# Edge network on one core: gathering three-part bf16 rows of h in place of rows of the first-layer table

## The chip, the cores and the metric

The kernel runs on one core of a Trainium2 chip (trn2). The metric is the device time of one execution in microseconds. The engines are TensorE (PE, with its weight loads as PEld), VectorE (DVE), ScalarE (ACT), GpSimd (POOL) and the DMA engines, whose transfers are issued from the queues of SyncE (SP), ScalarE and GpSimd.

## What is computed

12,500 nodes have 32 features each; 200,000 edges (src, dst), sorted by dst, have 16 attributes each.

```python
h = relu(layernorm(x))
x_p, x_f = h[src], h[dst]
fwd = concat([x_f, x_p, edge_attr], 1); bwd = concat([x_p, x_f, edge_attr], 1)
flow = relu(concat([fwd, bwd]) @ Wf1 + bf1) @ Wf2 + bf2
total = segment_sum(flow, concat([dst, src]))
x = x + relu(total @ Wn1 + bn1) @ Wn2 + bn2
h = relu(layernorm(x))
x = x + segment_sum(h[dst], src)
```

## The kernel before, in words

Edges are worked through in tiles of 128. Four tiles (U = 4) make a round, four rounds (R = 4) a window of 16 tiles, and there are NI = 104 windows, so 416 rounds. The first NTW = 98 windows bring new edges; the last six hold the tiles by which blocks of 128 nodes that share a tile are counted twice. A schedule, worked out on the chip, says for every tile which rows it takes and which block of nodes it belongs to.

**Start (up to about 150 us).** DVE normalises x into `h` (L1090 to L1104), finds out whether the edges are sorted (L1115 to L1131), makes one-hot digits for a histogram over src (L1150, L1152; PE sums them at L824) and then builds two schedules, k = 1 for dst and k = 0 for src. Each goes in four chunks of 416 columns: PE multiplies (L866, L867), DVE copies three results out (L1201 to L1203), PE may do the next chunk. A few passes over one row follow (L1206 on); `sched_done` tells the others. Beside that a table is built, block group by block group: ACT stages h (L724), PE transposes (L837), ACT copies (L729), PE multiplies with both halves of the first-layer weights (L846), ACT copies 512 columns (L739), SP stores (L374). The table `t2_rows` has one row of 128 float32 (512 bytes) for each node: what the node adds to the hidden layer when it is a source, for both directions. `h` is also split into three bf16 parts, hi, mid and lo, in `h3` (ACT L743, L746, L750; DVE subtracts at L1158 and L1223).

**Edge stage (about 150 to 4324 us).** For each round, SP loads the 128 indices of every tile and the attributes (L395, L397). GpSimd issues four indirect DMAs that gather the rows of `t2_rows` for src into `ring` (L610), and four that scatter the finished records to `records` (L620). Its order is written out: the gathers of round v + 2, then the scatters of round v. DVE makes the one-hot matrix of dst, two rounds ahead; PE transposes it (L914), ACT copies (L756), PE expands h of the dst nodes out of `h3` (L926), ACT copies into rows 0 to 95 of `cmb` (L762). The hidden layer is two float32 matmuls for each tile: the identity with the gathered rows (L943), and `cmb` (96 rows of dst, one of ones, 16 of attributes) with the weights `w3` (L944). ACT applies relu twice, to the half that is summed into dst (L773) and to the half that goes into the records (L778). PE counts positions (L955 to L959), DVE turns them into `pos` (L1275 to L1281), PE sums over dst (L972), DVE adds to `acc` (L1266).

**After it.** The records are read back in order of src and summed (4334 to about 5130 us, PE L1010), the node network runs, h of the second layer is stored to `h_rows` (SP L429), and GpSimd gathers 1568 tiles of its 128-byte rows (L674, 5223 to 7192 us), which PE sums into x (L1072).

The order around the change is set by semaphores. `gather_t2` may begin when the whole table is in DRAM (`t2_written`), `hist_ps` is 2 and `sched_done` is 2, since `ring` lies over the space of h, of the one-hots and of `e0f`. SP issues in its own order: all stores of the table, then the loads of the first edges.

Of the kernel before, what the change touches and what calls it, by code (L numbers as in the profile page):

```python
# [36 lines left out]
U = 4  # L37
# [21 lines left out]
assert NI % 8 == 0 and NTW % 8 == 2 and RG >= NB - 1 + 3 * U  # L59
# [36 lines left out]
def build(nc, x, sd, ea, w12_in, w3_in, wf2e_in, wn1_in, bn1_in, wn2_in, bn2_in, out):  # L96
    with ExitStack() as ctx:
# [17 lines left out]
        t2_rows = dram("t2_rows", [NBP * P, P])  # L115
# [25 lines left out]
        w12 = sb("w12", [P, U, P])  # L141
        w3 = sb("w3", [H3 + 1 + EA, P])
# [12 lines left out]
        ring = ring_flat.rearrange("p (t c) -> p t c", c=P)  # L155
# [3 lines left out]
        rest = ring_flat[:, 2 * LN_:RG * P]  # L159
        acc = sb("acc", [P, NBP, ACC])  # L160
# [24 lines left out]
        ln_tmp = acc_flat[:, B_:B_ + LN_].rearrange("p (b f) -> p b f", f=D)  # L185
# [53 lines left out]
        t2s = cmb_all[:, 0:2, :, :]  # L239
        before_b = ohd_h[:, :, :, :].rearrange("p k u n -> p (k u n)").bitcast(F32)  # L240
        hs, hT = (before_b[:, m * 2 * P:(m + 1) * 2 * P].rearrange("p (k n) -> p k n", k=2) for m in range(2))
# [39 lines left out]
        hs_ready, hsT_ready, hT_ready, tab_ready = sem("hs_ready"), sem("hsT_ready"), sem("hT_ready"), sem("tab_ready")  # L281
        t2s_ready, t2_written = sem("t2s_ready"), sems("t2_written", 2)
# [81 lines left out]
        def _(sp):  # L364
            sp.dma_start(nat[:, :, :], sd[0:E, :].rearrange("(p c) k -> p c k", p=NP)).then_inc(nat_in, 16)
            sp.dma_start(row_next[0:NP - 1, :], sd[0:E, :].rearrange("(p c) k -> p c k", p=NP)[1:NP, 0, :]).then_inc(nat_in, 16)
            for to, of in ((w12[:, :, :].rearrange("p u c -> p (u c)"), w12_in), (w3[:, :], w3_in), (wf2e[:, :], wf2e_in), (wn1[:, :], wn1_in),
                           (bn1c[:, :], bn1_in), (wn2[:, :, :].rearrange("p k f -> p (k f)"), wn2_in), (bn2r[:, :], bn2_in)):
                sp.dma_start(to, of).then_inc(w_in, 16)

            def store_t2(i, first, last):
                for k in range(2):
                    sp.wait_ge(t2s_ready, i * 2 + k + 1)
                    sp.dma_start(t2_rows[bass.ds((i * 2 + k) * (U * P), U * P), :].rearrange("(u p) f -> p u f", p=P),  # L374
                                 t2s[:, k, :, :]).then_inc(t2_written[k], 16)
            rounds_of(sp, NG // 2, store_t2)


            sp.wait_ge(sched_done, 1)
            sp.wait_ge(rearranged, 1)  # L380
            sp.wait_ge(by_d_copied, 16)
            sp.wait_ge(ea_first, 16)
# [4 lines left out]
            def load_edges(i, m, first, sources):  # L387
                if sources:
                    load_sources(i + 1, (m + 1) % 8)
                for r in range(R):  # L390
# [18 lines left out]
            for m in range(8):  # L409
                load_edges(NTW // 8 * 8 + m, m, False, m < NTW % 8 - 1)  # L410
# [37 lines left out]
            for k in range(2):  # L448
                sp.wait_ge(t2_written[k], 16 * (NG // 2))
# [99 lines left out]
        def _(pool):  # L549
# [38 lines left out]

# [7 lines left out]
            for k in range(2):  # L596
# [8 lines left out]
            def gather_t2(s, m, r):  # L605
# [3 lines left out]
                for u in range(U):  # L609
                    nc.gpsimd.indirect_dma_start(  # L610
                        out=ring[:, m * W + r * U + u, :], out_offset=None, in_=t2_rows,
# [21 lines left out]
            edges(0, 9)  # L633
            with pool.Fori(1, NTW // 8) as s:
                edges(s, 9)
# [57 lines left out]
        def _(act):  # L693
# [25 lines left out]
            def stage_h(i, k, first):  # L719

                if not first:
                    act.wait_ge(hsT_ready, i * 2 + k - 1)
                    act.sem_inc(act_tick, 1)
                nc.scalar.activation(hs[:, k, :].rearrange("p (u f) -> p u f", u=U), h[:, bass.ds((i * 2 + k) * U, U), :], ACT.Copy).then_inc(hs_ready, 1)  # L724

            def tables(i, first, last):
                for k in range(2):
                    act.wait_ge(hsT_ready, i * 2 + k + 1)
                    nc.scalar.activation(hT[:, k, :], pb[k][:, 0:P], ACT.Copy).then_inc(hT_ready, 1)  # L729
                if not last:  # L730
                    for k in range(2):
                        stage_h(i + 1, k, False)
                for k in range(2):
                    act.wait_ge(tab_ready, i * 2 + k + 1)
                    act.sem_inc(act_tick, 1)
                    if not first:
                        act.wait_ge(t2_written[k], 16 * i)
                        act.sem_inc(act_tick, 1)
# [765 lines left out]
```

## Time and profile before

| | us |
|---|---|
| median of 3 runs | 9138.04 |
| lowest and highest run | 9131.39, 9163.98 |
| span of the profiled execution, first to last instruction | 7224.1 |
| GpSimd busy in the span | 5197.9 (72%) |
| PE busy | 4419.8 (61%) |
| DVE busy | 3200.3 (44%) |
| ACT busy | 1352.3 (19%) |

The profiled execution has no device time of its own beside its span. The median of the runs stands 1913.9 us above the span; no view says what lies there. In the views a row of a timeline is start, duration, engine, line, operation, destination<-sources and count; in brackets stands the idle time before it and what ended it.

### The profile page before, as it was taken

The page shows a single profiled execution, that of the slowest core. Times are in us where ns is not written, and L with a number is a line of the kernel's source. Part 1 is how long each engine was busy: PE and PEld are TensorE (multiplying, and loading weights), DVE is VectorE, ACT ScalarE, POOL GpSimd, SP SyncE. Part 2 cuts the span into 40 slices and gives each one's busy share as a digit, 9 for nine tenths or more (in the row PEclk, how much of TensorE's full clock was granted, in tenths as well). Part 3 has the DMA queues.
Part 4 walks back from the last instruction along what each step waited for, and adds up shares of the span by engine and source line. Part 5 has one row for each costly group of instructions (what it writes and reads, how often), then busy time and mean ns, then how long its engine had stood idle before and what let it go on. Part 6 is the DMA issues. An engine that isn't in the chain of part 4 may idle for free.

```text
span 7224.1 us, 127054 instructions
## 1 busy us (share of the span) xinstructions
PE 4419.8 (61%) x23241; PEld 3987.8 (55%) x23244; DVE 3200.3 (44%) x15358; ACT 1352.3 (19%) x4288; POOL 5197.9 (72%) x5767
## 2 busy tenths in 40 slices
PE   4666666666666666666666679999733333333333
PEld 3655556555555655555565569999533333333333
DVE  5444444444444444444444466666523232323232
ACT  2222222222222222222222234434200000000000
POOL 2777777777777777777777766666377777777776
PEclk8666676666766666766667785555655555555555
DMA  5222222222222222222222123333111111111111
GB/s 154 43 46 43 43 43 43 43 42 43 42 43 43 42 43 42 42 42 42 43 42 42 41 35 73 71 71 73 30 14 14 14 14 14 14 14 14 14 14 20
DMA packets 1109393, 290.45 MB, mean 40 GB/s; under 512 B 992782, under 2 KB 1058701, under 8 KB 1108518
## 3 DMA queue, kind: packets, MB, share of 16 engines
q0 software_dynamic: 153824, 183.68, 10.7%
q1 hardware_dynamic: 954758, 88.54, 10.3%
q10 hardware_dynamic: 576, 16.16, 0.7%
q14 instruction: 216, 1.77, 0.1%
q8 instruction: 19, 0.31, 0.0%
HBM read 223.49 MB, written 82.32 MB: 42 GB/s over the span
## 4 chain that ended last, share of the span: by engine, by line
POOL 59%; issue 27%; DVE 6%; PE 3%; DVEq 2%; DMA 2%; POOLq 0%; ACT 0%; ACTq 0%; SPq 0%
POOL records L620 21%; POOL ring L674 20%; POOL ring L610 18%; DVE acc L1266 3%; DVEq L331 1%; PE bank L1010 1%; DVE oht L1337 1%; DVE ohd L1337 1%; DVEq L1266 1%; DMA ring<-records 0%; PE bank L943 0%; PE bank L846 0%; DMA row_next<-in_sd 0%; PE bank L944 0%; PE bank L972 0%
## 5 line engine op out<-in xcount | busy, mean ns | idle before, releaser
L620 POOL DMA_INDIRECT records<-rec,pos x1664 | 1650.3, 992 | 526.7 <-issue 507.8
L674 POOL DMA_INDIRECT ring<-h_rows,didx x1568 | 1491.1, 951 | 576.3 <-issue 477.5
L610 POOL DMA_INDIRECT ring<-t_rows,sidx x1568 | 1519.5, 969 | 484.9 <-issue 482.1
L943 PE MATMUL bank<-ring,ident 128*128 x3328 | 1094.3, 431 | 1254.6 <-DMA ring<-t_rows,sidx 1249.8
L943 PEld LDWEIGHTS bank<-ring,ident 128*128 128x128 f32 x3328 | 868.4, 320 | 1309.9 <-issue 1309.8
L1072 PE MATMUL bank<-ring,ohd 128*128 x1664 | 376.2, 402 | 1282.8 <-POOLq L684 1282.2
L1072 PEld LDWEIGHTS bank<-ring,ohd 128*128 128x128 f32 x1664 | 362.9, 330 | 1295.9 <-issue 1295.9
L1275 DVE TENSOR_TENSOR prod<-bank,q_row 128x392 f32<-128x392 f32 x416 | 235.7, 567 | 1895.8 <-PE bank L959 1895.6
L944 PE MATMUL bank<-w,cmb 113*128 113x128 f32 x3328 | 1026.2, 411 | 0.0
L1266 DVE TENSOR_TENSOR acc<-acc,bank 128x65 f32 x3328 | 734.6, 221 | 524.9 <-issue 279.1
L1266 DVE TENSOR_TENSOR xs<-xs,bank 128x32 f32 x1664 | 304.3, 183 | 1384.2 <-PE bank L1072 1371.3
L944 PEld LDWEIGHTS bank<-w,cmb 113*128 113x128 f32 x3328 | 883.0, 324 | 0.0
L773 ACT ACTIVATE rf<-bank 128x256 f32<-128x256 f32 x416 | 159.8, 384 | 2735.3 <-PE bank L944 2733.2
L972 PE MATMUL bank<-rf,ohd 128*128 128x65 f32 x3328 | 453.1, 279 | 9.7 <-ACT rec L778 0.3
L972 PEld LDWEIGHTS bank<-rf,ohd 128*128 128x128 f32 x3328 | 407.9, 193 | 54.4 <-issue 3.1
L1010 PE MATMUL bank<-ring,ohd 128*128 x1664 | 381.7, 421 | 62.4 <-POOL ohd L654 62.0
L1010 PEld LDWEIGHTS bank<-ring,ohd 128*128 128x128 f32 x1664 | 362.9, 330 | 80.7 <-issue 80.7
L802 ACT CAST raw<-ring (+1 forms) x1664 | 312.4, 192 | 478.6 <-DMA ring<-records 337.5
L1010 PE MATMUL bank<-ring,oht 128*128 x1664 | 382.3, 418 | 6.4 <-issue 6.4
L1010 PEld LDWEIGHTS bank<-ring,oht 128*128 128x128 f32 x1664 | 369.2, 332 | 10.7 <-issue 10.6
L1072 PE MATMUL bank<-ring,oht 128*128 x1664 | 374.5, 401 | 0.0
L1072 PEld LDWEIGHTS bank<-ring,oht 128*128 128x128 f32 x1664 | 367.4, 333 | 0.0
(213 smaller groups left out, 6508.9 us busy)
## 6 DMA issues: line engine op xcount, KB each, us to landing
ring<-records SPq DMA_DIRECT2D x104, 536.0 KB, 4.3
rec_i<-by_d_sd SPq DMA_DIRECT2D x1664, 1.0 KB
cmb<-by_d_ea SPq DMA_DIRECT2D x1664, 8.0 KB
records<-rec,pos POOLq DMA_INDIRECT x1664
ring<-t_rows,sidx POOLq DMA_INDIRECT x1568
ring<-h_rows,didx POOLq DMA_INDIRECT x1568, 2.4
by_d_ea<-in_ea ACTq DMA_DIRECT2D x8, 1579.0 KB, 19.1
t_rows<-cmb SPq DMA_DIRECT2D x26, 256.0 KB, 2.2
```

The costliest lines, as they stand in the source:

```text
L610: nc.gpsimd.indirect_dma_start(out=ring[:, m * W + r * U + u, :], out_offset=None, in_=t2_rows, in_offset=bass.IndirectOffsetOnAxis(ap=sid ...
L620: nc.gpsimd.indirect_dma_start(out=records, out_offset=bass.IndirectOffsetOnAxis(ap=pos[:, r, u:u + 1].bitcast(U32), axis=0), in_=rec[:, r ...
L674: nc.gpsimd.indirect_dma_start(out=h2g[:, w * W + t, :], out_offset=None, in_=h2_rows, in_offset=bass.IndirectOffsetOnAxis(ap=didx[:, k, t ...
L773: nc.scalar.activation(rf[:, :, 0:HID], pre[:, :, 0:HID], ACT.Relu)
L802: ins = nc.scalar.copy(pairs[:, bass.ds(j0 + u, 1), :].rearrange("p a k -> p (a k)"), srec[w][:, bass.ds(at[u], 1), HID + 1:REC].bitcast(I ...
L943: nc.tensor.matmul(p, ident[:, :], ring[:, bass.ds(at[u], 1), :].rearrange("p a c -> p (a c)"), start=True, stop=False)
L944: ins = nc.tensor.matmul(p, cmb[:, r, u, :], w3[:, :], start=False, stop=True)
L972: ins = nc.tensor.matmul(pb[3][:, u * ACC:(u + 1) * ACC], ohd[:, r % 2, u, :], rf[:, u, :], start=True, stop=True)
L1010: ins = nc.tensor.matmul(s_bank[r][:, u * ACC:(u + 1) * ACC], s_oh[r][:, u, :], srec[w][:, bass.ds(at[r * U + u], 1), 0:ACC].rearrange("p ...
L1072: ins = nc.tensor.matmul(s_bank[r][:, u * D:(u + 1) * D], s_oh[r][:, u, :], h2g[:, bass.ds(at[r * U + u], 1), :].rearrange("p a f -> p (a ...
L1266: return nc.vector.tensor_tensor(to, to, src[:, u * width:(u + 1) * width], ALU.add)
L1275: placed = chain.link(nc.vector.tensor_tensor(prod[:, :, :], q[:, 0:U, :], bcast_mid(q_row[:, r % 2, :], U), ALU.add))
```

## The change

The table, its weights `w12`, its loop on ACT, PE and SP and its two scratch tiles go. `h3` itself is stored to DRAM as `h3_rows` (96 bf16, 192 bytes a node), each of its three parts by its own DMA as soon as it is split off. GpSimd gathers rows of `h3_rows` into `hring`. PE transposes the four gathered tiles of a round with the bf16 identity into bank 5, ACT copies them into rows 0 to 95 of `cmb` (with the ones and the attributes), and the expanded h of dst goes into a tile of its own, `cmb_dst`. The hidden layer is `cmb_dst` with `wdst` and `cmb` with `wsrc`. GpSimd's order is the scatters of round v, then the gathers of round v + 4 (`LEAD`); the source indices are loaded two windows ahead. It waits for `h3_written` in place of the table and `sched_done`. In the schedule ACT takes the copy of `base_row`, and `blk` is made in one pass over it. On DVE the digits come ahead of the wait for the deviation, the subtractions lie between the one-hots, and the memset of `acc` no longer waits for `lo_ready`.

```diff
-            def store_t2(i, first, last):
...
+            sp.wait_ge(rearranged, 1)
+            sp.wait_ge(by_d_copied, 16)
             load_sources(0, 0)
-            for k in range(2):
-                sp.wait_ge(t2_written[k], 16 * (NG // 2))
+            load_sources(1, 1)
+            for k, part_ready in enumerate((hi_ready, mid_ready, lo_ready)):
+                sp.wait_ge(part_ready, 1)
+                sp.dma_start(h3_rows.rearrange("(b p) f -> p b f", p=P)[:, :, k * D:(k + 1) * D], h3[:, :, k * D:(k + 1) * D]).then_inc(h3_written, 16)
+            sp.wait_ge(sched_done, 1)
+            sp.wait_ge(ea_first, 16)
...
-            for k in range(2):
-                pool.wait_ge(t2_written[k], 16 * (NG // 2))
...
-            pool.wait_ge(mid_ready, 1)
             pool.wait_ge(hist_ps, 2)
-            pool.wait_ge(sched_done, 2)
+            pool.wait_ge(h3_written, 48)
...
-                        m2, r2 = m + (r + 2) // R, (r + 2) % R
+                        m2, r2 = m + (r + LEAD) // R, (r + LEAD) % R
+                        scatter_records(s * 8 + m, r)
                         if m2 < gathers:
-                            gather_t2(s + m2 // 8, m2 % 8, r2)
-                        scatter_records(s * 8 + m, r)
-            gather_t2(0, 0, 0)
-            gather_t2(0, 0, 1)
+                            gather_h3(s + m2 // 8, m2 % 8, r2)
+            for g in range(LEAD):
+                gather_h3(0, g // R, g % R)
...
             nc.scalar.activation(h3[:, :, 0:D], h, ACT.Copy).then_inc(hi_ready, 1)
-            span(act, 1, 8, tables)
             act.wait_ge(r1_ready, 1)
-            nc.scalar.activation(h3[:, :, D:2 * D], ln_tmp, ACT.Copy).then_inc(mid_ready, 1)
...
+            nc.scalar.activation(h3[:, :, D:2 * D], h, ACT.Copy).then_inc(mid_ready, 1)
             act.wait_ge(r2_ready, 1)
+            nc.scalar.activation(h3[:, :, 2 * D:H3], h, ACT.Copy).then_inc(lo_ready, 1)
+            for n, k in enumerate((1, 0)):
+                for c in range(J // JC):
+                    act.wait_ge(sched_ps, n * (J // JC) + c + 1)
+                    nc.scalar.activation(base_row[k][:, c * JC:(c + 1) * JC], pb[6][:, 0:JC], ACT.Copy).then_inc(base_copied, 1)
...
+                act.wait_ge(srcT_ps, v)
+                act.sem_inc(act_tick, 1)
+                nc.scalar.activation(cmb[0:H3, r, :, :].rearrange("p u n -> p (u n)"), pb[5][0:H3, :], ACT.Copy)
                 act.wait_ge(hd_ps, v)
                 act.sem_inc(act_tick, 1)
-                nc.scalar.activation(cmb[0:H3, r, :, :].rearrange("p u n -> p (u n)"), pb[1][0:H3, :], ACT.Copy).then_inc(cmb_ready, 1)
+                nc.scalar.activation(cmb_dst[:, r % 2, :, :].rearrange("p u n -> p (u n)"), pb[1][0:H3, :], ACT.Copy).then_inc(cmb_ready, 1)
...
+            def transpose_sources(i, r, gathered):
+                at = four(pe, gs_row, i * W + r * U, RG - 1)
                 if gathered:
                     pe.wait_ge(gat[r], 16 * U * (i + 1))
                     pe.sem_inc(pe_tick, 1)
+                for u in range(U):
+                    ins = nc.tensor.matmul(pb[5][0:H3, u * P:(u + 1) * P], hring[:, bass.ds(at[u], 1), :].rearrange("p a c -> p (a c)"), ident_h[:, :],
+                                           start=True, stop=True)
+                ins.then_inc(srcT_ps, 1)
...
-                    nc.tensor.matmul(p, ident[:, :], ring[:, bass.ds(at[u], 1), :].rearrange("p a c -> p (a c)"), start=True, stop=False)
-                    ins = nc.tensor.matmul(p, cmb[:, r, u, :], w3[:, :], start=False, stop=True)
+                    nc.tensor.matmul(p, cmb_dst[:, r % 2, u, :], wdst[:, :], start=True, stop=False)
+                    ins = nc.tensor.matmul(p, cmb[:, r, u, :], wsrc[:, :], start=False, stop=True)
...
+                    if not last or r < R - 1:
+                        transposes(j, k)
+                        transpose_sources(j, k, more)
                     counts(i, r, first)
...
-                    nc.vector.tensor_copy(base_row[k][:, s], pb[6][:, 0:JC])
-                    nc.vector.tensor_scalar(blk[k][:, s], pb[6][0:1, 0:JC], 1.0 / P, None, ALU.mult)
                     nc.vector.tensor_copy(e0f[:, s], pb[7][0:1, HCOL:HCOL + JC]).then_inc(sched_read, 1)
                 dve.wait_ge(sched_read, (n + 1) * (J // JC))
+                dve.wait_ge(base_copied, (n + 1) * (J // JC))
+                own.link(nc.vector.tensor_scalar(blk[k][:, :], base_row[k][0:1, :], 1.0 / P, None, ALU.mult))
...
-            dve.wait_ge(lo_ready, 1)
             own.step(nc.vector.memset(acc[:, :, :], 0.0))
```

## Rows read from the trace of the kernel before

**Rows 1.** The page: shares of the chain that ended last, and GpSimd's three groups.

```profile
POOL 59%; issue 27%; DVE 6%; PE 3%; DVEq 2%; DMA 2%; POOLq 0%; ACT 0%; ACTq 0%; SPq 0%
...
L620 POOL DMA_INDIRECT records<-rec,pos x1664 | 1650.3, 992 | 526.7 <-issue 507.8
L674 POOL DMA_INDIRECT ring<-h_rows,didx x1568 | 1491.1, 951 | 576.3 <-issue 477.5
L610 POOL DMA_INDIRECT ring<-t_rows,sidx x1568 | 1519.5, 969 | 484.9 <-issue 482.1
```

**Rows 2.** Waits over the span: engine, tile and line, us in total, times, longest.

```profile
PE bank L943 <- DMA ring<-t_rows,sidx: 1249.8, 390, 4.9
...
POOL records L620 <- DVE pos L1281: 18.9, 11, 2.8
```

**Rows 3.** Timeline, GpSimd: first gather and scatter, last gather and scatter.

```profile
149.84 3.51 POOL L610 DMA_INDIRECT ring<-t_rows,sidx  x1 [7.34 <-issue]
...
167.62 1.04 POOL L620 DMA_INDIRECT records<-rec,pos  x1 [0.30 <-issue]
...
4163.92 1.23 POOL L610 DMA_INDIRECT ring<-t_rows,sidx  x1 [0.30 <-issue]
...
4322.86 0.98 POOL L620 DMA_INDIRECT records<-rec,pos  x1 [0.30 <-issue]
```

**Rows 4.** Timeline, tail: two rounds of PE at full clock without gathers.

```profile
4279.13 0.48 PE L943 MATMUL bank<-ring,ident 128*128 x2
...
4284.53 0.48 PE L943 MATMUL bank<-ring,ident 128*128 x2
```

**Rows 5.** Groups by line: what the added steps are most like.

```profile
L914 PE MATMUL bank<-ident_h,ohd_h 128*128 128x128 bf16 x1664 | 247.8, 299 | 13.6 <-DVE ohd_h L1248 13.4
...
L762 ACT ACTIVATE cmb<-bank 96x512 f32<-96x512 f32 x416 | 246.8, 593 | 445.9 <-PE bank L926 430.1 <-issue 15.7
```

**Rows 6.** Timeline of the start, DVE, ACT and PE.

```profile
47.81 0.21 DVE L1133 TENSOR_SCALAR stat<-stat 128x104 f32<-128x104 f32 x1
...
54.91 0.15 DVE L1135 CAST first_f<-first_i 125x1 f32<-125x1 int32 x1 [6.88 <-DMA first_i<-by_d_sd]
...
56.11 3.62 DVE L1103 TENSOR_TENSOR ring<-ring,stat 128x3328 f32<-128x3328 f32 x1
59.77 1.90 DVE L1104 TENSOR_SCALAR ring<-ring 128x3328 f32<-128x3328 f32 x1
61.58 0.99 DVE L1138 TENSOR_SCALAR acc<-raw 125x1600 int32<-125x1600 int32 x1
...
65.95 3.68 DVE L1150 TENSOR_SCALAR ring<-acc 125x800 bf16<-125x800 bf16 x13
...
67.30 2.97 ACT L743 ACTIVATE h<-ring 128x3328 bf16<-128x3328 f32 x1
...
84.17 4.98 PE L824 MATMUL bank<-acc,ring 125*104 125x64 bf16 x100
```

**Rows 7.** Timeline, DVE: the two schedules and the first round.

```profile
96.58 0.15 DVE L1168 COPY edge_col<-start_col 98x1 f32<-98x1 f32 x1 [7.64 <-PE bank L879]
...
138.29 0.59 DVE L1201 COPY wide<-bank 128x416 f32<-128x416 f32 x1 [2.04 <-PE bank L867]
...
140.78 0.59 DVE L1201 COPY wide<-bank 128x416 f32<-128x416 f32 x1 [0.71 <-PE bank L867]
...
142.60 1.88 DVE L1206 SCALAR_TENSOR_TENSOR ring<-jrow,ring 1x1664 f32<-1x1664 f32 x1
...
152.40 0.17 DVE L1238 CAST sdf<-rec_i 128x8 f32<-128x8 int32 x1
...
158.31 5.69 DVE L1319 MEMSET acc<- 128x6760 f32 x1 [1.36 <-issue]
```

**Rows 8.** Windows (busy by engine, clock, DMA share, GB/s) and DMA issues (KB, landing us).

```profile
70.00:80.00 10.00, 6.16 (x29) 5.92 (x30) 9.96 (x29) 2.96 (x12) 8.60 (x1) 0.68 0.69 201
...
h_rows<-ring SPq DMA_DIRECT2D x1, 1664.0 KB, 13.2
```

More of the change, by code:

```diff
@@ L58 @@
 NTW = TW
-assert NI % 8 == 0 and NTW % 8 == 2 and RG >= NB - 1 + 3 * U
+assert NI % 8 == 0 and NTW % 8 == 2
 assert E % 125 == 0 and JC <= 512 and J % 4 == 0 and NI % SW == 0 and TW < NI - SW and EP >= TW * W * P and EP // P - W < TW * W
@@ L447, in _ @@
             sp.wait_ge(h2_written, 16)
-            for k in range(2):
-                sp.wait_ge(t2_written[k], 16 * (NG // 2))
+            sp.wait_ge(h3_written, 48)
         FB_STEPS = 15
@@ L833, in _ @@
             pe.wait_ge(wflow_ready, 1)
-            def transpose_h(i, k):
-                pe.wait_ge(hs_ready, i * 2 + k + 1)
-                nc.tensor.transpose(pb[k][:, 0:P], hs[:, k, :], ident[:, :]).then_inc(hsT_ready, 1)
-            def tables(i, first, last):
-                for k in range(2):
-                    if not first:
-                        pe.wait_ge(t2s_ready, i * 2 + k - 1)
-                        pe.sem_inc(pe_tick, 1)
-                    pe.wait_ge(hT_ready, i * 2 + k + 1)
-                    for u in range(U):
-                        ins = nc.tensor.matmul(pb[2 + k][:, u * P:(u + 1) * P], hT[:, k, :], w12[:, u, :], start=True, stop=True)
-                    ins.then_inc(tab_ready, 1)
-                if not last:
-                    for k in range(2):
-                        transpose_h(i + 1, k)
             def tile_counts(k):
@@ L928, in expand @@
                 ins.then_inc(hd_ps, 1)
-            def hidden(i, r, gathered):
-                v = i * R + r + 1
+            def transpose_sources(i, r, gathered):
                 at = four(pe, gs_row, i * W + r * U, RG - 1)
@@ L973, in sums, with edges @@
                 ins.then_inc(sum_ready, 1)
-            def edges(i, first, last, gathered=True):
+            def edges(i, first, last, gathered=True, next_gathered=True):
                 for r in range(R):
-                    hidden(i, r, gathered)
-                    if r < R - 1:
-                        transposes(i, r + 1)
-                    elif not last:
-                        transposes(i + 1, 0)
+                    hidden(i, r)
+                    j, k, more = (i, r + 1, gathered) if r < R - 1 else (i + 1, 0, next_gathered)
+                    if not last or r < R - 1:
+                        transposes(j, k)
+                        transpose_sources(j, k, more)
                     counts(i, r, first)
-                    if r < R - 1:
-                        expand(i, r + 1)
-                    elif not last:
-                        expand(i + 1, 0)
+                    if not last or r < R - 1:
+                        expand(j, k)
                     sums(i, r, first)
             pe.wait_ge(ones_set, 1)
+            pe.wait_ge(sched_read, 2 * (J // JC))
+            pe.wait_ge(base_copied, 2 * (J // JC))
+            pe.wait_ge(sched_done, 2)
             transposes(0, 0)
+            transpose_sources(0, 0, True)
             pe.wait_ge(lo_ready, 1)
@@ L1477 @@
     x[0:N] = inputs["x"]
-    w12 = np.zeros((P, U, P), np.float32)
-    for u in range(U):
-        w12[u * D:(u + 1) * D, u, :] = np.concatenate([second, first], axis=1)
-    as_dst = np.concatenate([first, second], axis=1)
+    as_src, as_dst = np.concatenate([second, first], axis=1), np.concatenate([first, second], axis=1)
     twice = np.concatenate([w["bf1"], w["bf1"]])[None, :]
```

130 lines of the change are left out of this document (43 added, 87 removed).

## The prediction

> **What bounds the kernel now.** I read the chain that ended last first, then the groups behind it. GpSimd holds 59% of the chain, and "issue", the 0.3 us between two of its DMAs, most of the next 27%; its three groups of indirect DMAs cost about 0.97 us each plus about 0.31 us of issue [rows 1]. The waits say who waits in the edge stage: PE waits 1249.8 us in 390 rounds, 3.2 us a round, for gathered rows, while GpSimd waits 18.9 us in all for positions [rows 2]. The timeline gives the period: from the first scatter at 167.62 to the last gather at 4163.92 GpSimd does 389 rounds, 10.27 us each, or 1.28 us for each of eight DMAs [rows 3]. So 4 ms of the span hang on how many indirect DMAs GpSimd issues, whatever they carry; 149.84 us lie before the first gather and 158.7 us after the end of the last one (4165.15 to 4323.84), where PE is the bound again: 25 rounds, 6.3 us each, 5.40 at full clock [rows 3, 4].
>
> The number of gathers (1568) and scatters (1664) stays. The change can win only at the start, in the order around it and at the tail, and can lose on the price of one gather or on PE.
>
> **GpSimd's DMAs.** A row shrinks from 512 to 192 bytes. The rows of 128 bytes at L674 cost 951 ns each, those of 512 bytes 969, those of 268 bytes, scattered, 992 [rows 1]. 192 bytes lie among them. I take no change; the ends are -18 ns and +23 ns times 1568, so -28 and +36 us.
>
> **The round on PE and ACT.** Removed: the identity matmul on gathered rows. Added: a float32 matmul of 96 rows in its place (same columns, taken as equal), four bf16 transposes, 0.60 us a round as L914's 247.8 us over 416, and an ACT copy of 0.59 us as L762 [rows 5]. Both together on the chain are 1.2 us, against 3.2 us that PE waits [rows 2]. The cover is GpSimd's period; without it, in the tail, the price shows. There ACT idles 445.9 us over 416 rounds, 1.07 us each, just ahead of the copy for PE's expansion [rows 5], and that is where the new copy goes; PE has the like gap in front of the expansion. So I take zero for the tail, with +0.7 us times 25 rounds = +17 us as the upper end. PE now waits for the gather of round v inside round v - 1, ahead of counts and sums of v - 1; with four rounds of lead GpSimd comes to the scatters of v - 1 some 25 us after that gather, so the wait has nobody behind it. DVE's round, SP's 32 edge loads of a window and the one load of indices stay; they are only issued earlier.
>
> **The order.** Before, 12 gathers stand ahead of the first scatter and 389 rounds of eight follow it. Now 16 stand ahead of it and 388 rounds follow. From the first scatter to the last gather that is one period less: -10.3 us. The tail from the last gather on is set by PE, which starts round 391 then in either case, so its 158.7 us stay.
>
> **The start.** Two chains lead to the first scatter, now at 167.62.
>
> The schedule. DVE is free at 48.0; four digit passes at 0.99 us fill its wait for the deviation and the first edges (which let it go at 54.91), reciprocal and scaling (0.8 + 3.6) follow, the two small passes of `lt`, then relu 1.9: h is ready at 59.0, against 61.7 [rows 6]. ACT's hi copy takes 2.97: 62.2. First subtraction 3.6, one-hots 3.68 + 2.31 = 6.0, second subtraction 3.6 (mid is ready by 69), one-hots 6.0: 81.5. PE's second histogram, 5.0 us [rows 6], ends at 86.6, and the first column of the schedule is read at 86.9 in place of 96.58 [rows 7]. The small operations to the first chunk take 4.4 us without the table between them: 91.3. A chunk takes 2.49 us now, with three DVE copies of 0.59 [rows 7]; two leave, so 1.35, and four take 5.4: 96.7. The ACT copy of `base_row` runs beside the remaining one. The single pass for `blk` (1.0) and three passes (3.9): 101.6. The second schedule: 2.6 + 4.4 for its columns, 5.4 for its chunks, 1.0 for `blk`, and 6.25 of passes (142.60 to 148.85, where the 3.6 us subtraction stood before the loads of the first round at 152.40): 121.3. That is 27.6 us ahead of 148.85. From there the first two rounds' one-hots 4.5, the memset of acc 5.7 without the 1.36 us of wait [rows 7], and 2.1 for the positions: first scatter at 133.6.
>
> The stores. Three stores wait for hi (62.2), mid (69) and lo (78.5). Until about 78 the attribute copies fill the DMA engines (share 0.69 over 70 to 80), so hi hardly moves before. The nearest row is the store of the second layer's h, as many pieces (13,312) of 128 bytes, 13.2 us [rows 8]. At that price three end at 78 + 39.6 = 118. The first gather takes 3.5 us and fifteen more 1.25 each: GpSimd would reach the first scatter at 140. If a piece of half the size cost 60% (8 us), they would end at 102 and the schedule would decide, 133.6. I take 137, nearer to the row than the cheap end is.
> The Trainium skill, "DMA: Bandwidth & Descriptors", section "Why small descriptors are slow", gives a piece a fixed 3 cycles beside one for each 32 bytes: 5 cycles for 64 bytes, 7 for 128, so as an estimate 9.4 us a store; by that the stores end at 106, and the sum would be 3 us better than mine.
>
> GpSimd's own gather for the schedule (L592, rows of the edge list) now starts near 59.5, free of the one-hots, and is not late. The 26 table stores leave SP's queue, and SP's first edge loads stand behind the three big stores: if SP is held until lo is nearly written, they land near 120, just when DVE wants them. That is inside the 3 us I added.
>
> **Sum.** First scatter 167.6 to 137: -30.6. One round less after it: -10.3. Gathers, PE, tail: 0. Together -41 us: span 7183. The execution behind the rows has a span of 7224.1, 1913.9 us below the median of the runs, 9138.0; no view shows those microseconds, and I carry them over unchanged: 9097 us, -0.45%.
>
> **The rivals.**
> The stores are the start. A 64-byte piece could cost twice the 128-byte one: 26.4 each, 79 us, ending at 157; first scatter 179, 11 us later than now, and the round won pays it back: 9138, no change. For it: sub-copies of only 64 bytes have no row. Against: the 128-byte row moves 1664 KB in 13.2 us, 129 GB/s, under the 201 GB/s that the row of 70 to 80 us shows, so pieces already hold it and not bytes.
> The Trainium skill, same page, opening table, wants 512 bytes for a DMA and says that below it the engine reads, modifies and writes; by that rule both the 64-byte stores and the 192-byte gathers are the wrong way, and this rival is its outcome. No row here shows a doubling: the 128-byte gathers cost GpSimd no more than the 512-byte ones [rows 1]. 10%.
>
> The unseen time follows the bytes. 1914 us are 0.40 us for each of 4800 indirect DMAs. If they are moved bytes, weights 1568 x 512, 1664 x 268 and 1568 x 128 become 1568 x 192 in the first: 65% of before, -662 us, time 8435. Against: DMA engines are idle for four fifths of the stage in the profile. 8%.
>
> Slower: PE's round becomes the bound. If the unseen time lies in PE's and ACT's chain of the edge stage (4.6 us a round over 416), then the added transposes count in full, 0.60 x 416 = +250 us, and with the copy +495: 9347 to 9592. It decides when the chain, 10.27 - 3.2 = 7.1 us in the profile and 8.3 after, passes 10.27. For it: PE's clock stands between its two levels, and half clock lengthens every matmul. Against: 2 us of room in the profile. 7%.
>
> That the change does not do what it says I see no way for: the table, its loop and the chunk copies are plainly gone.
>
> **Chances.** A measurement of this kernel can tell about 0.5%, 46 us. The forecast has 75%; its -41 lies just inside that bound, and its terms spread to either side (gathers -28 to +36, stores -3 to +3, tail 0 to +17, runs 16 us apart), so it gives 0.37 faster, 0.35 same, 0.03 slower. The stores give 0.08 same, 0.02 slower; the unseen bytes 0.08 faster; PE 0.07 slower. Together faster 0.45, same 0.43, slower 0.12. The range takes the forecast with the gathers' cheap end and some of the runs' spread, 9045, and on the other side the stores' rival with the runs' spread, 9160; the two large rivals, 15%, lie outside.
>
> **What would show it.** Right: first gather near 115, first scatter near 137, 10.27 us a round in between, about 159 us from the end of the last gather to that of the last scatter, PE's wait moved from the hidden layer to the transposes and near 2.5 us a round. Wrong: a gather above 1.0 us; first gather past 125; GpSimd waiting for positions or relu in the middle of the stage; a tail round above 7 us; or a span that falls by 41 us while the median does something else.

## The result and the profile after

| | median us | runs | span of its profiled execution | its own time |
|---|---|---|---|---|
| before | 9134.72 | 9119.58 to 9163.98 (4) | | |
| after | 9216.57 | 9198.88 to 9231.15 (4) | 9228.1 | 9229.7 |

The ratio is 1.0079, 95% interval 1.0055 to 1.0104: 82 us slower, where -41 was forecast and 9045 to 9160 allowed. The first thing to see is in the table: the span of the changed kernel is its time, within 2 us. Nothing lies outside it. The 1914 us that the profiled execution of before lacked were in no hidden place; here they stand inside the span.

The timeline of after, GpSimd alone, first gather and scatter, last gather and scatter (start us, us; in brackets the idle time before and its releaser):

```profile
112.43 1.00 POOL L597 DMA_INDIRECT ring<-h_rows,sidx  x1 [50.88 <-DMA h_rows<-h]
...
141.49 1.03 POOL L607 DMA_INDIRECT records<-rec,pos  x1 [5.28 <-DVE pos L1229]
...
5654.14 0.95 POOL L597 DMA_INDIRECT ring<-h_rows,sidx  x1 [0.30 <-issue]
...
5901.28 0.98 POOL L607 DMA_INDIRECT records<-rec,pos  x1 [0.30 <-issue]
```

Against [rows 3] the start is as forecast (first gather 112.4 for 115, first scatter 141.5 for 137), and everything after it is longer: 388 rounds of 14.21 us where before had 389 of 10.27. The groups of after say that it isn't the DMAs (busy us, mean ns of one | idle before, by releaser):

```profile
L607 POOL DMA_INDIRECT records<-rec,pos x1664 | 1649.5, 991 | 2139.9 <-DVE pos L1229 1597.5 <-issue 542.5
L597 POOL DMA_INDIRECT ring<-h_rows,sidx x1568 | 1522.6, 971 | 528.7 <-issue 477.8 <-DMA h_rows<-h 50.9
...
L873 PE MATMUL bank<-ident_h,ring 128*96 128x128 bf16 x1664 | 259.7, 300 | 56.5 <-issue 53.2
...
L727 ACT ACTIVATE cmb<-bank 96x512 f32<-96x512 f32 x416 | 246.3, 592 | 393.5 <-remote 314.7 <-PE bank L873 45.2 <-issue 29.2
```

A gather takes 971 ns for 969 and a scatter 991 for 992 [rows 1]. The added transposes take 260 us and the copy 246, as costed. What is new is 1597.5 us in which GpSimd waits for positions; it was 18.9 [rows 2]. The waits of after:

```profile
DVE prod L1223 <- remote: 2315.5, 319, 13.1
...
POOL records L607 <- DVE pos L1229: 1597.5, 301, 10.5
ACT rf L741 <- remote: 1462.0, 153, 18.5
```

So DVE, which makes the positions, waits for the counts of PE, and GpSimd waits for DVE. The experiments had to say whether the change did this.

### The profile page after: what moved, and what is told of

It reads as the page before. It is cut to its first block and busy times, and to the rows that moved or that the text cites. A ratio compares the mean times of both kernels' runs of the same rounds, so it can differ in the third digit from the quotient of the medians.

```text
span 9228.1 us, 130413 instructions
## 1 busy us (share of the span) xinstructions
PE 4739.6 (51%) x24671; PEld 4305.7 (47%) x24674; DVE 3202.2 (35%) x15344; ACT 1577.5 (17%) x4634; POOL 5199.1 (56%) x5767
## 5 line engine op out<-in xcount | busy, mean ns | idle before, releaser
L607 POOL DMA_INDIRECT records<-rec,pos x1664 | 1649.5, 991 | 2139.9 <-DVE pos L1229 1597.5
L597 POOL DMA_INDIRECT ring<-h_rows,sidx x1568 | 1522.6, 971 | 528.7 <-issue 477.8
L886 PE MATMUL bank<-wdst,ring 96*128 96x128 f32 x3328 | 1089.7, 430 | 1240.7 <-ACT ring L730 959.5
L886 PEld LDWEIGHTS bank<-wdst,ring 96*128 96x128 f32 x3328 | 884.6, 325 | 1269.0 <-issue 1268.9
L887 PE MATMUL bank<-wsrc,cmb 113*128 113x128 f32 x3328 | 1037.6, 415 | 0.0
L887 PEld LDWEIGHTS bank<-wsrc,cmb 113*128 113x128 f32 x3328 | 894.4, 328 | 0.0
L1018 PEld LDWEIGHTS bank<-ring,ohd 128*128 128x128 f32 x1664 | 365.8, 329 | 926.2 <-issue 926.2
L1018 PE MATMUL bank<-ring,oht 128*128 x1664 | 393.0, 402 | 765.0 <-issue 574.3
L862 PE MATMUL bank<-oht,h 128*96 128x128 bf16 x1664 | 277.9, 297 | 969.6 <-ACT oht L721 709.9
L1018 PEld LDWEIGHTS bank<-ring,oht 128*128 128x128 f32 x1664 | 372.5, 330 | 780.5 <-issue 780.3
L862 PEld LDWEIGHTS bank<-oht,h 128*96 x1664 | 209.2, 140 | 1049.3 <-issue 1037.2
L730 ACT ACTIVATE ring<-bank 96x512 f32<-96x512 f32 x416 | 246.3, 592 | 1284.1 <-remote 987.4
## 6 DMA issues: line engine op xcount, KB each, us to landing
h_rows<-h SPq DMA_DIRECT2D x3, 832.0 KB, 21.4
```

The lines of the kernel that those rows point to most:

```text
L597: nc.gpsimd.indirect_dma_start(out=hring[:, m * W + r * U + u, :], out_offset=None, in_=h3_rows, in_offset=bass.IndirectOffsetOnAxis(ap=si ...
L607: nc.gpsimd.indirect_dma_start(out=records, out_offset=bass.IndirectOffsetOnAxis(ap=pos[:, r, u:u + 1].bitcast(U32), axis=0), in_=rec[:, r ...
L730: nc.scalar.activation(cmb_dst[:, r % 2, :, :].rearrange("p u n -> p (u n)"), pb[1][0:H3, :], ACT.Copy).then_inc(cmb_ready, 1)
L862: ins = nc.tensor.matmul(pb[1][0:H3, u * P:(u + 1) * P], h3[:, bass.ds(at[u], 1), :].rearrange("p a c -> p (a c)"), oht_h[:, r % 2, u, :], ...
L886: nc.tensor.matmul(p, cmb_dst[:, r % 2, u, :], wdst[:, :], start=True, stop=False)
L887: ins = nc.tensor.matmul(p, cmb[:, r, u, :], wsrc[:, :], start=False, stop=True)
```

## The experiments

The runs come in groups; those of one group ran on the same chip, beside the kernel before. Each recorded expectation stands ahead of its result; it says "call" for such a group.

**The kernel before once more, and parts of the change, first group.** b_same is the kernel before. a_no_srct takes from the changed kernel three things: the transposition of gathered rows, the register load that PE needs for it, and ACT's copy; it leaves the sources' part out of the hidden layer (ones stand there). a_order2 and b_order4 exchange the order of GpSimd's DMAs, and b_order4 loads the source indices two windows ahead, as the changed kernel does. The edits are shown without their lesser lines (...).

```diff
# a_no_srct, after without
-            nc.gpsimd.memset(cmb[H3:H3 + 1, :, :, :], 1.0).then_inc(ones_set, 1)
+            nc.gpsimd.memset(cmb[0:H3 + 1, :, :, :], 1.0).then_inc(ones_set, 1)
...
-                act.wait_ge(srcT_ps, v)
-                act.sem_inc(act_tick, 1)
-                nc.scalar.activation(cmb[0:H3, r, :, :].rearrange("p u n -> p (u n)"), pb[5][0:H3, :], ACT.Copy)
...
-                at = four(pe, gs_row, i * W + r * U, RG - 1)
...
-                for u in range(U):
-                    ins = nc.tensor.matmul(pb[5][0:H3, u * P:(u + 1) * P], hring[:, bass.ds(at[u], 1), :].rearrange("p a c -> p (a c)"), ident_h[:, :],
-                                           start=True, stop=True)
-                ins.then_inc(srcT_ps, 1)
# a_order2, after with
+                        if m2 < gathers:
+                            gather_h3(s + m2 // 8, m2 % 8, r2)
                         scatter_records(s * 8 + m, r)
-                        if m2 < gathers:
-                            gather_h3(s + m2 // 8, m2 % 8, r2)
...
-LEAD = 4
+LEAD = 2
# b_order4, before with the scatter ahead of the gather, LEAD = 4 and load_sources(i + 2, (m + 2) % 8)
```

> The kernel before, profiled once more. The profile of the kernel after has a span of 9228 us with gaps on all queues that the profile of before (span 7224 us, median of the runs 9135 us) does not show. Theory 1 (the 1914 us are ordinary stalls that one lucky execution lacked): a span near 9130 us, GpSimd waiting for positions in the edge stage for 1000 us or more, and an edge stage of 5600 us or more in place of 4174. Theory 2 (the stalls came with the change): a span near 7224 us again, without such waits.

> The kernel after, without the transposition of the gathered rows and without its copy by ScalarE (rows 0 to 95 of cmb hold ones, so the sources' part of the hidden layer is left out). Theory 1 (the chain of PE and ScalarE is the bound of the edge stage, and each added step counts): 1.0 to 1.2 us less in each of 416 rounds, so 400 to 500 us below after, and some 320 to 420 below before. Theory 3 (GpSimd is the bound, the chain has room): within 30 us of after.

> The kernel after with GpSimd's order of before: gathers of round v + 2, then scatters of round v. Theory 1 (chain with stalls, GpSimd waits in 300 rounds): less lead takes room away from the chain, since PE waits for a gather in the middle of the round before: 100 to 400 us slower than after. Theory 3 (GpSimd is the bound): 10 us slower than after, the one round of lead.

> The kernel before with GpSimd's order of after alone: scatters of round v, then gathers of round v + 4, source indices loaded two windows ahead; the table stays. Theory 1 (chain with stalls): four rounds of lead let GpSimd absorb stalls: 50 to 300 us faster than before. Theory 3 (GpSimd is the bound): 5 to 10 us faster than before.

This group showed another speed. The kernel before took 7239.11 us, and so did b_same (ratio 1.0001 [0.9991, 1.0010], span 7218.9). a_no_srct: 1.0001 [0.9992, 1.0011]; a_order2: 0.9997 [0.9988, 1.0007]; b_order4: 0.9993 [0.9984, 1.0003]. So the same program takes 7.2 ms in one group and 9.1 in another, with spans that equal the times in either. I call these the first and the second kind. Theories 2 and 3 had the numbers right here, and yet the groups below show that the kind decided and not the kernel. The span of [rows 1], 7224, is one of the first kind; the result is one of the second.

**The changed kernel on a second chip.** a_same is the changed kernel.

> The kernel after, once more, beside the kernel before on the same chip. Theory 1a (two kinds of execution conditions: with stalls of all queues the kernel before takes 9135 us and the chain of PE and ScalarE bounds the edge stage; without them it takes 7239 us and GpSimd does): where before takes about 7239 us, after takes 7215 to 7265 us, within 0.4% of it, with its first scatter near 140 us, since the 24 us won at the start are given back in the tail or in GpSimd's own time; where before takes about 9135 us, after is again 50 to 110 us slower. Theory 2 (the change itself is slower by 82 us): after is 82 us, 1.1%, slower under either condition.

9194.10 against 9123.81: 1.0087 [1.0071, 1.0103]. Second kind, and the loss repeats.

**Both kernels and two parts on a third chip.** b_again is before, a_again after.

> The kernel before, profiled beside the others of this call. If this chip runs it in about 9130 us: GpSimd waits for positions in 250 rounds or more, the edge stage takes 5500 to 5700 us, its tail after the last gather 210 to 240 us, and all queues show common gaps. If in about 7239 us: as before, none of these.

> After without the transposition and its ScalarE copy, again. Where before takes about 9130 us: by theory 1 (the chain of PE and ScalarE bounds the edge stage there, each added step counts) 250 to 500 us below after, so 180 to 430 below before; by theory 4 (stalls come with the DMAs and the chain has room between them) 0 to 100 us below after. Where before takes 7239 us: within 0.2% of before, as in the first run.

> Before with four rounds of lead, again. Where before takes about 9130 us: by theory 1 50 to 300 us faster than before, since the lead takes up stalls; by theory 5 (the new order is the loss) 50 to 100 us slower than before. Where before takes 7239 us: within 0.2% of it, as in the first run.

> The kernel after. Where before takes about 9130 us: 60 to 90 us slower, as in the two comparisons so far. Where before takes 7239 us: 7215 to 7265 us, with GpSimd's gathers at 0.97 to 1.00 us and the tail after the last gather 10 to 25 us longer than the 159 us of before.

First kind: b_again 7222.6, before 7221.09. a_again took 7210.95, 0.9984 [0.9974, 0.9993]: here the change is a gain of 0.16%. a_no_srct_2: 1.0007 [0.9997, 1.0016], although it has less to do: its gathers took 996 ns each in place of 969, 42 us over 1568. b_order4_2: 0.9992 [0.9983, 1.0002]. The timeline of a_again:

```profile
110.33 1.00 POOL L597 DMA_INDIRECT ring<-h_rows,sidx  x1 [49.07 <-DMA h_rows<-h]
...
139.64 1.04 POOL L607 DMA_INDIRECT records<-rec,pos  x1 [6.08 <-ACT rec L746]
...
4120.61 0.94 POOL L597 DMA_INDIRECT ring<-h_rows,sidx  x1 [0.30 <-issue]
...
4301.20 0.98 POOL L607 DMA_INDIRECT records<-rec,pos  x1 [0.30 <-issue]
```

388 rounds of 10.26 us, as forecast, and PE's wait is at the transposes, 2.1 us a round. In b_again the first scatter stands at 163.2 and the tail takes 158.8 us; here they are 139.6 and 180.6. The two profiles differ by -23.5 at the start, -17.4 from the first scatter to the last gather (one round of 10.3 less, and 0.02 us less in each of the others), +21.8 in the tail and +4.7 behind it: -14, where the medians say -10. The tail is PE's. Its rounds in a_again's timeline, last gathers gone:

```profile
4257.59 0.39 PE L887 MATMUL bank<-wsrc,cmb 113*128 113x128 f32 x2
...
4260.94 0.62 PE L873 MATMUL bank<-ident_h,ring 128*96 128x128 bf16 x4 [0.44 <-issue]
...
4261.68 0.59 ACT L727 ACTIVATE cmb<-bank 96x512 f32<-96x512 f32 x1 [0.55 <-PE bank L873]
...
4263.34 0.59 ACT L730 ACTIVATE ring<-bank 96x512 f32<-96x512 f32 x1 [1.06 <-PE bank L862]
...
4264.43 0.39 PE L887 MATMUL bank<-wsrc,cmb 113*128 113x128 f32 x2
```

6.84 us from hidden layer to hidden layer, where before had 5.40 at full clock [rows 4]; in the mean 7.2 us, where before had 6.3. PE stands 0.44 us "issue" ahead of L873: there the engine loads the ring's slot into a register, which the change put between the two groups of transposes. How much of the tail that is can be read from the windows of the two tails (us, PE, PEld, DVE, ACT and POOL busy, granted clock, DMA share, GB/s) and from PE's waits in them, b_again first:

```profile
4162.44:4321.21 158.77, 125.10 (x942) 109.74 (x942) 113.67 (x541) 57.24 (x147) 106.42 (x108) 0.90 0.14 26
...
PE bank L926 <- ACT oht L756: 16.7, 24, 0.8
```

```profile
4121.56:4302.17 180.61, 146.77 (x1066) 127.48 (x1065) 115.69 (x546) 75.07 (x178) 110.42 (x112) 0.87 0.13 24
...
PE bank L873 <- issue: 7.9, 18, 0.5
PE bank L850 <- DVE ohd_h L1196: 7.7, 18, 0.9
PE bank L862 <- issue: 6.6, 18, 0.5
```

PE is idle for 33.7 us in the one tail and 33.8 in the other, and busy for 21.7 us more: the whole growth is busy time, 15.9 us of it the added transposes. The gap ahead of the expansion (L926 before, L862 after) did shrink, from 16.7 to 7.4 us in all, but new ones opened ahead of the two groups of transposes: 7.9 us for the register load and 7.7 for DVE's one-hots. Without transposes, copy and load the tail takes 148.6 us (a_no_srct_2).

The windows of the edge stage of before, then of a_again show one more thing, and the rounds, 10.27 and 10.26 us, show no cost of it: with the change the clock of the edge stage is 0.53, nearly always the lower level, for 0.69.

```profile
300.00:4100.00 3800.00, 2556.51 (x14050) 2225.74 (x14049) 1713.49 (x8137) 870.04 (x2220) 2898.36 (x2959) 0.69 0.22 43
```

```profile
300.00:4100.00 3800.00, 3006.59 (x15556) 2685.43 (x15557) 1708.92 (x8157) 1090.38 (x2590) 2897.15 (x2963) 0.53 0.18 27
```

**The same on a fourth chip, and the register load.** b_again2 is before; a_early is after with that load ahead of the hidden layer's matmuls.

```diff
+                    if not last or r < R - 1:
+                        at = four(pe, gs_row, j * W + k * U, RG - 1)
                     hidden(i, r)
                     if not last or r < R - 1:
                         transposes(j, k)
-                        transpose_sources(j, k, more)
+                        transpose_sources(j, k, more, at)
```

> The kernel before, for a profile on a chip that runs it in about 9130 us, if this is one. Then: edge stage to about 5800 us (5867.6 in the profile of after, less some 66), GpSimd waiting for positions in 250 rounds or more, gaps on all queues; a tail round near 8 us in place of 8.7. Else a span near 7220 us with a tail of 159 us, as three times before.

> After without the transposition of gathered rows and its ScalarE copy. Where before takes about 9130 us: theory 1 (added steps lengthen the chain in the rounds in which it is the bound, about 300 to 370 of 416, by the 1.0 us that the tail's round shows) 250 to 400 us below after; theory 4 (the chain has room between stalls) less than 100 us below after. Where before takes about 7220 us: within 0.2% of before, with a tail of 149 us.

> Before with the new order and four rounds of lead. Where before takes about 9130 us: theory 1 says the lead takes up stalls and wins 50 to 300 us; theory 5 (the order is the loss) 50 to 100 us slower. Where before takes about 7220 us: within 0.2% of it, as twice.

> After, with TensorE's register load for the gathered rows' slots moved ahead of the hidden layer's matmuls, where it stood before the change; at its new place it leaves TensorE idle for 0.45 us in each round. Theory 6 (that load is the larger part of the longer tail round, 6.4 in place of 5.4 us at full clock): tail 10 to 15 us shorter than after's 181 us, so 0.3 to 0.4% below before where before takes 7220 us; where it takes 9130 us, 100 to 200 us below after by theory 1, 0 to 30 by theory 4.

Second kind: b_again2 9136.81 (before 9118.13), and so at last a profile of before to set beside that of after. Its waits:

```profile
DVE prod L1275 <- remote: 1700.1, 287, 9.1
...
POOL records L620 <- DVE pos L1281: 1501.7, 282, 9.4
```

GpSimd waits 1501.7 us for positions in the kernel **before** too, in 282 rounds. The missing 1914 us, b_again2 against [rows 3]: edge stage from first to last scatter +1491, second layer's gathers +334, end +81, start +6. The change is on top. a_no_srct_3: 0.9910 [0.9888, 0.9933]; b_order4_3: 0.9994 [0.9978, 1.0011]; a_early: 1.0051 [1.0032, 1.0071]. Transposition, copy and register load together make the whole loss and more: 69 us below before without them, 70 above with them (a_same, another chip), by the medians. That is 140 us, less than the 250 to 400 of theory 1 and more than the 100 of theory 4. The order makes none of it, and theory 1's gain from more lead did not come. The load's idle time is gone in a_early (0.6 us ahead of the transposes in all, 56.5 in after); that its place is worth perhaps 30 us is not shown, since a_early and a_same ran on two chips and their intervals touch.

**The transposition behind the counts, and more small loads.** a_mid is a_early with the transposition of the gathered rows behind the counts; b_dbl is before with SP's four 8-byte-row loads of a round issued twice, the second time into a tile that nobody reads.

```diff
# a_mid
                         transposes(j, k)
-                        transpose_sources(j, k, more, at)
                     counts(i, r, first)
                     if not last or r < R - 1:
+                        transpose_sources(j, k, more, at)
                         expand(j, k)
# b_dbl
...
+                    for u in range(U):
+                        sp.dma_start(rec_2[:, r, u, :], by_d_sd[bass.ds(at[u], P), :]).then_inc(twice[r], 16)
```

> After with the register load moved ahead of the hidden layer's matmuls and the transposition of the gathered rows moved behind the counts, into TensorE's wait for ScalarE's copy of the one-hot matrix. Theory 6 (in after the two lengthen the round by their place more than by their work): tail round at full clock back to 5.4 to 5.6 us from 6.4. Where before takes about 9120 us: 60 to 150 us below after, so 0 to 0.8% below before. Where it takes about 7220 us: tail 155 to 165 us, 25 to 35 us below before. If the work itself is the cost (theory 1 in its plain form), the tail round stays above 6.2 us and the time within 30 us of after.

> The kernel before with every load of the 8-byte edge indices issued a second time into a scratch tile (512 more pieces of 8 bytes in a round, DMA packets 1.11 to 1.96 million). Theory 7 (the gaps of all queues come with SP's loads in 8-byte pieces): where before takes about 9120 us, 500 us or more slower; where it takes 7220 us, within 40 us of before, since SP has room. Theory 8 (the gaps come from elsewhere): less than 150 us slower under either condition.

Second kind. a_mid: 9037.57, 1.0016 [1.0006, 1.0025], so most of the loss hung on what stands ahead of the counts in PE's queue. Which of the three steps moved there is the dear one, the four transposes, PE's wait for the gather or the later copy on ACT, no run separates. b_dbl: 1.0075 [1.0058, 1.0093]: +67 us for 1664 DMAs more (1.35 million packets in place of 1.11, not the 1.96 of its expectation). The loads aren't what makes 1914 us.

**Who is late.** The trace answers this without a run. One round of b_again2 (second kind), rows of PE, DVE and ACT:

```profile
2993.70 0.64 PE L944 MATMUL bank<-w,cmb 113*128 113x128 f32 x2
...
3000.97 0.70 PE L959 MATMUL bank<-ohs,ones_h 128*128 128x294 bf16 x3
...
3003.96 0.38 ACT L773 ACTIVATE rf<-bank 128x256 f32<-128x256 f32 x1 [13.17 <-remote]
3004.10 0.57 DVE L1275 TENSOR_TENSOR prod<-bank,q_row 128x392 f32<-128x392 f32 x1 [2.84 <-remote]
```

The like of it in b_again (first kind):

```profile
3006.73 0.64 PE L944 MATMUL bank<-w,cmb 113*128 113x128 f32 x2
3007.40 0.38 ACT L773 ACTIVATE rf<-bank 128x256 f32<-128x256 f32 x1 [6.61 <-PE bank L944]
...
3008.24 0.70 PE L959 MATMUL bank<-ohs,ones_h 128*128 128x294 bf16 x3
3008.98 0.57 DVE L1275 TENSOR_TENSOR prod<-bank,q_row 128x392 f32<-128x392 f32 x1 [4.76 <-PE bank L959]
```

In the latter the hidden layer's record ends at 3007.37 and ACT begins 0.03 us later; counts and DVE likewise. In the former the hidden layer's record ends at 2994.34 and ACT begins at 3003.96 (it waits there for the sums as well, which let DVE go at 2998.24); the counts' record ends at 3001.67 and DVE begins 2.43 us later. Over 350 rounds the delay from the counts' record to DVE is 0.04 us in b_again, 3.8 in b_again2 and 4.7 in after. The trace also holds the updates of semaphores, with gaps. In b_again2, from 474 us to the last gather, those of ACT and DVE come 0.01 us after their instruction in the median. Those of PE come late: 4.6 us for the hidden layer, 3.2 for the transposes, 3.9 for the counts and 0.7 for the expansion, all 0.01 us in b_again. The ends of matmuls are modelled in such a trace, so either PE finishes later than its records say, or its signals are held; the trace can't part the two. In the stage that sums the records, without indirect DMAs, PE's signals come 0.01 us after their records in both kinds; in the second layer's gathers they are late again (1.4 us in the median against 0.01), at a granted clock of 0.50 in both.

**Two theories of that delay.** b_pe8 adds eight matmuls of the added form, twice the change's, without a copy. b_first and a_first put the counts of a round ahead of its hidden layer.

```diff
# b_pe8, before with
+                    for u in range(2 * U):
+                        nc.tensor.matmul(pb[5][0:H3, (u % U) * P:(u % U + 1) * P], h3[:, 0, :], ident_h[:, :], start=True, stop=True)
                     counts(i, r, first)
# b_first (before) and a_first (a_mid)
+                    counts(i, r, first)
                     hidden(i, r)
                     transposes(j, k)
-                    counts(i, r, first)
```

> The kernel before with eight matmuls of the added form (96 columns of weights, 128 columns of data, bfloat16, no signal, nobody waits for them) put into every round ahead of the counts, which is twice what the change adds, and no copy by ACT. Theory 9: on chips of the second kind (9 ms) TensorE really finishes its matmuls 3 to 5 us later than their records say, in the two stages in which GpSimd issues indirect DMAs, so that its work is on the path there: +120 to +300 us on such a chip (twice the added transposes, 2 x 0.60 x 416 = 500 us at most), and the delay from the last count's record to DVE's L1275 grows from 3.6 us. On a chip of the first kind (7.2 ms) nothing within 0.2% (GpSimd's period covers 1.2 us), tail round of PE 6.6 us in place of 5.4. Rival: the transposes cost nothing by themselves and ACT's copy of them, which this kernel lacks, is what the change lost: no change within 0.2% on either kind.

> The kernel before with the counts of a round put ahead of its hidden layer on PE. They are then ready while DVE still adds the sums of the round before. Theory 9a: on chips of the second kind what is late is only the path from PE's counts to DVE (a latency behind the hidden layer's float32 matmuls): the delay from the count's record to DVE falls below 1 us and the kernel gains 200 us or more there. Theory 9b: TensorE as a whole lags and its throughput is the bound: within 50 us of before, the delay moves to the hidden layer's and the sums' readers. On a chip of the first kind: no change within 0.2% either way, with the 18.9 us of waits for positions gone.

> The changed kernel with the register load of the ring's slot ahead of the round and the counts put ahead of the hidden layer. Theory 9a: gains 200 us or more against before on a chip of the second kind. Theory 9b: within 50 us of the kernel before (a_mid, with the counts between, was 14.5 us slower than before there). On a chip of the first kind: 0.1 to 0.3% faster than before (7200 to 7213 us), as the start gains 24 us, the order 10 us, and the tail loses less than the 22 us of the changed kernel.

The chip has the number of the first group's, where before took 7239; now it takes 9033.31. The kind doesn't belong to the number. b_pe8: 9060.12, 1.0029 [1.0017, 1.0042]: matmuls alone cost 27 us for eight a round, far under the 120 expected, although the delay from the counts' record to DVE did grow, to 6.7 us. The rival in its expectation, by which ACT's copy is what the change lost, said none at all; it is nearer, but no run has the copy without the transposes. b_first: **8799.37, 0.9745 [0.9731, 0.9758]**; a_first: 8856.74, 0.9806 [0.9793, 0.9820]. Both beat both kernels of this case. The waits of b_first:

```profile
ACT rf L773 <- remote: 3791.6, 395, 10.9
DVE acc L1266 <- issue: 3412.7, 591, 11.2
...
POOL records L620 <- ACT rec L778: 1178.3, 388, 4.0
```

DVE hardly waits for counts any more: it takes them up 1.9 us after their record, since it adds the sums until then, and idles 0.06 us ahead of them. But the delay has moved, to ACT's wait for the hidden layer, 4.8 us a round after its record, and GpSimd waits for ACT's records. PE's signals say the same: those of the hidden layer and of the transposes behind it come 4.8 and 4.6 us late in b_first, those of the counts ahead of it 0.55 (169 of 366 recorded) and those of the expansion 0.01. In b_pe8 the hidden layer's come 0.01 us late (129 of 367 recorded), and the counts', the expansion's and the sums', all behind the eight matmuls, 6.2 to 7.0. A round of b_first takes 13.15 us, not 10.27. So theory 9a, for b_first, priced the gain rightly (234 us of the 200 or more; 177 for a_first, under it) and is wrong that only the counts are late; 9b is wrong that moving them brings nothing. What is late is a part of PE's queue, up to the next of its waits, and what matters is who waits behind it. The change costs in this order too: a_first is 57 us above b_first, and its round is 13.40 us.

## Why the prediction was wrong

**"No view shows those microseconds, and I carry them over unchanged."** This step failed. They weren't a constant beside the span but idle time inside it, in runs of the second kind, most of it GpSimd waiting for the chain PE, DVE, GpSimd. The profile read was of the first kind, the median to be forecast of the second. A span 21% below every timed run should have been read as a profile of another kind of run, in which each "cover" has to be asked for anew.

**"The cover is GpSimd's period."** True in the first kind: 10.26 us a round with the change. Even there the kernel gained 10 us and not 41, by the start (-23.5 for -30.6) and the tail (+21.8 for 0). In the second GpSimd waits for positions, the cover is gone and PE's order shows. Spans of after (9228.1) and b_again2 (9135.2), two chips of that kind, differ by 93 us: start -32.5, rounds 388 x 14.21 - 389 x 13.91 = +101, tail 247.2 - 235.2 = +12, the later stages +12. That is the rival "PE's round becomes the bound". Its place was right, its price (+250 to +495) two to four times too high: a round grew by 0.30 us and not by 0.60 to 1.19.

**The stores and the start.** Right within 5 us: first gather 112.4 for 115, first scatter 141.5 for 137, -26.1 for -30.6. The sum took 13.2 us for each from [rows 8]. Queued behind one another the three show a median of 21.4 from issue to landing (DMA issues of after):

```profile
h_rows<-h SPq DMA_DIRECT2D x3, 832.0 KB, 21.4
```

The three were issued between 75.7 and 89.0 and landed at 90.7, 100.8 and 111.4, so 10.0 and 10.7 us apart; the last one let GpSimd go at 112.4, 6 us before the sum's 118.
The estimate by the Trainium skill, "DMA: Bandwidth & Descriptors", "Why small descriptors are slow", was 9.4 us a store and ended them at 106; the measured end lies halfway between that and 118. The Trainium skill, opening table of the same page, has a DMA of under 512 bytes read, modified and written, and the rival took that for twice the price; no run shows a doubling, the stores came 10 to 11 us apart and the 192-byte gathers took 971 ns.

**Gathers.** Right: 0 forecast, +2 ns each measured, 3 us over 1568.

**The order, -10.3.** Borne out in size by the first kind (a_again 0.9984, a_order2 0.9997, 9 us apart, on two chips) and not on before's side (b_order4 -0.07% and -0.08%, each interval reaching zero). In the second kind it brings nothing, since GpSimd isn't the bound.

**The tail, 0 with +17 as the end.** Wrong even in the first kind: +21.8. The copy does lie in a gap of ACT, but "PE has the like gap in front of the expansion" failed as a reason for zero. PE's idle time in the tail stayed the same (33.8 us for 33.7) and its busy time grew by 21.7, so the transposes counted in full. What the gap ahead of the expansion gave (9 us), new gaps took back; half of these is the register load for the ring's slot (7.9 us), which moved with the transposition to the middle of PE's round and isn't in the prediction's list of added steps.

**What would show it.** Of the signs against it two came: GpSimd waiting for positions in the middle of the stage, and a tail round above 7 us (7.2 in a_again, 9.9 in after).

## What to carry to other kernels

When a profile's span isn't the time of the runs, find out first where the rest is: profile again until the span is the time, and read there what bounds the kernel. An addition that is free under another engine's period is only as free as that period is the bound; here the same edit was -0.16% in one kind of run and +0.79% in the other. And the order of an in-order queue is worth as much as its content: to put the counts, for which a chain of engines waits, ahead of the hidden layer took 2.5% off the kernel before in the second kind, three times what the whole change moved; in the first kind it was not run.

## What was unexpected of the hardware

The same program took 7221 to 7239 us in some groups of runs and 9023 to 9135 in others, a quarter more, each group of one kind throughout, and one chip number was once of each. In the second kind PE's results come 3 to 5 us a round later than its records end, and only in the stages in which GpSimd issues indirect DMAs. In b_first the full clock is granted for 1488 us of the edge stage, in 389 stretches of 3.4 or 6.8 us; only 21 of PE's recorded signals fall into them, all but one of these more than 4 us after the start of a stretch. In the kernel before, in the first kind, 942 fall into 1474 us. But the second layer shows the delay at a constant 0.50. Whether PE is held back then, and by what, stays open: no run took the clock or the indirect DMAs away. That a_no_srct's gathers took 996 ns for 969 is open as well.
